# Spare TensorE products in two stretches of a decoder block: an S4D convolution by Fourier products, cross attention, and a gated and expert feed-forward

## The reference

```python
# 1. S4D: a long convolution, by Fourier transforms of length 2048
K = 2 * real(einsum('hn,hnl->hl', Ct, exp(dtA * l)))       # taps, 256 channels x 1024
y = irfft(rfft(x, 2048) * rfft(K, 2048))[:, :1024]
r = x + (y + x * D)
x = layernorm(x + layernorm(r) * ln_w + ln_b)
# 2. cross attention, 16 heads of 16 channels, 77 keys per sequence
x = layernorm(x + softmax(q @ k.T * HD**-0.5) @ v @ Wo.T + bo)
# 3. gated feed-forward (256 -> 1024 -> 256) plus 1024 experts chosen by product keys
mlp = (silu(x @ Wg + bg) * (x @ Wu + bu)) @ Wd + bd
experts = sum over 4 heads and 8 choices of silu(x . down) * softmax(score) * up
x = layernorm(x + mlp + experts)
```

## Time and profile before

| | |
|---|---|
| median of three runs | 738.25 us (733.1 to 738.47) |
| the profiled execution | 737.21 us |
| its span, first to last instruction | 735.4 us |
| TensorE (products) busy | 635.6 us, 86% of the span |
| VectorE busy | 506.9 us, 69% |
| ScalarE busy | 407.0 us, 55% |
| GpSimd busy | 263.6 us, 36% |
| granted TensorE clock, mean | 0.896 of full speed |
| DRAM read and written | 25.47 MB and 13.63 MB |

### The profile page before, as it was taken

One profiled execution on the slowest core, in us unless ns is written; L12 is line 12 of the kernel. 1 busy time (PEld: TensorE's weight loads), 2 busy tenths in 40 slices (PEclk: granted clock), 3 DMA queues, 4 the chain that ended last, 5 costly groups with the idle time before them and its releaser, 6 DMA issues.

```text
span 735.4 us, 8935 instructions
## 1 busy us (share of the span) xinstructions
PE 635.6 (86%) x2724; PEld 425.6 (58%) x2724; DVE 506.9 (69%) x1051; ACT 407.0 (55%) x613; POOL 263.6 (36%) x337
## 2 busy tenths in 40 slices
PE   5698379893849687899999999999999999999996
PEld 2398244581737355554567765567765558654485
DVE  7999937340414578778785787786687877766783
ACT  4852335512113333568875487875487876478660
POOL 0030000075423233554334364334364235445261
PEclk9755579997878755799999999999999999999999
DMA  8909914838990700000000000000000000000000
GB/s 249 353 11 107 112 11 116 159 115 156 118 228 1 285 0 1 0 2 1 0 1 1 0 16 8 7 2 0 1 16 8 8 1 0 8 14 8 0 8 21
DMA packets 31162, 39.67 MB, mean 54 GB/s; under 512 B 3069, under 2 KB 24139, under 8 KB 30091
## 3 DMA queue, kind: packets, MB, share of 16 engines
q1 hardware_dynamic: 26730, 34.91, 22.4%
q10 hardware_dynamic: 4384, 4.20, 1.9%
HBM read 25.47 MB, written 13.63 MB: 53 GB/s over the span
## 4 chain that ended last, share of the span: by engine, by line
PE 61%; DVE 19%; DMA 8%; ACT 5%; issue 4%; SPq 1%; POOL 1%; DVEq 0%; ACTq 0%; POOLq 0%
PE bank L761 19%; PE bank L849 7%; PE bank L854 7%; DMA arena<-scr_x 5%; PE bank L804 3%; PE bank L826 3%; PE bank L783 3%; PE bank L816 3%; PE bank L792 2%; DVE stats L1349 2%; PE bank L648 2%; DVE arena L1440 1%; PE bank L841 1%; PE bank L651 1%; ACT arena L1064 1%
## 5 line engine op out<-in xcount | busy, mean ns | idle before, releaser
L1155 POOL TENSOR_TENSOR arena<-arena 128x1024 f32<-128x1024 f32 x64 | 125.6, 1962 | 157.1 <-ACT arena L1064 156.0
L761 PE MATMUL bank<-arena 128*128 128x512 f32 x384 | 174.5, 596 | 5.9 <-issue 3.6
L761 PEld LDWEIGHTS bank<-arena 128*128 128x128 f32 x384 | 70.0, 190 | 83.6 <-issue 76.6
L1064 ACT ACTIVATE arena<-arena 128x1024 f32<-128x1024 f32 x64 | 73.5, 1149 | 7.5 <-DVE arena L1438 3.2
L1066 ACT ACTIVATE arena<-arena 128x1024 f32<-128x1024 f32 x64 | 73.5, 1149 | 2.1
L1440 DVE SCALAR_TENSOR_TENSOR arena<-arena 128x1024 f32<-128x1024 f32 x48 | 63.8, 1330 | 1.7
L849 PE MATMUL bank<-arena 128*128 128x256 f32 x256 | 58.4, 381 | 2.5 <-DVE tok L1476 1.2
L1330 DVE TENSOR_TENSOR arena<-arena,bank 128x512 f32<-128x512 f32 x36 | 23.1, 684 | 50.4 <-PE bank L651 33.8
L854 PE MATMUL bank<-arena 128*128 128x256 f32 x256 | 57.9, 379 | 0.0
L954 ACT COPY arena<-bank 128x512 f32<-128x512 f32 (+1 forms) x64 | 34.0, 532 | 42.6 <-PE bank L753 30.2
L849 PEld LDWEIGHTS bank<-arena 128*128 128x128 f32 x256 | 47.5, 190 | 10.3 <-issue 3.3
(11 more groups left out here) (182 smaller groups left out, 1221.3 us busy)
## 6 DMA issues: line engine op xcount, KB each, us to landing
scr_x<-arena SPq DMA_DIRECT2D x16, 256.0 KB, 8.0
arena<-scr_x SPq DMA_DIRECT2D x8, 512.0 KB, 21.7
arena<-scr_z SPq DMA_DIRECT2D x32, 128.0 KB, 7.4
scr_z<-arena ACTq DMA_DIRECT2D x14, 256.0 KB, 4.1
tok<-in_x SPq DMA_DIRECT2D x8, 256.0 KB, 5.9
scr_k<-arena SPq DMA_DIRECT2D x4, 512.0 KB, 4.0
arena<-scr_k SPq DMA_DIRECT2D x16, 128.0 KB, 5.7
out<-tok SPq DMA_DIRECT2D x16, 128.0 KB, 1.7
```

Of the source, the lines that this page charges most:

```text
L761: ins = mm(bk[:, :], w[:, k, P * m:P * m + P], src[:, k, :], start=(k == 0), stop=(k == KC - 1))
L1064: fn(ebuf[m % 2], sxb[m % 2], ACT.Prelu, bias=negt[:, n % 2, h:h + 1], alpha=FAR).then_inc(s_ranked, 1)
L1155: tt(sxb[m % 2], sim[:, n % 2, h, 0:XR].unsqueeze(2).broadcast_to((P, XR, NKEYS)), sim[:, n % 2, FH + h, :].unsqueeze(1).broadcast_to((P, ...
```

## The change

Two places get products whose results nobody reads. `keep_busy(bk, count)` issues `count` products of `wq[:, 0, 0:128]` with `wq[:, 1, :]` (128 rows, 128 by 256 columns) into the given PSUM bank.

1. In the second half of the taps' spectra (`hf` is 1) each `k_second` and each `inverse` begins with two of them, ahead of its waits, in bank 4. That makes 18 places with 36 products.
2. `with_busy` puts a step "busy" in front of each `score`, `probs`, `attend`, `turno` and `project` of tiles 0 to 3. That makes 32 steps with three products each, 96 in all. Each takes a unit of the wide ring; it is free again when TensorE itself has finished the step.

```diff
+def with_busy(steps):
+    busy = []
+    for y in steps:
+        if y[0] in ("score", "probs", "attend", "turno", "project") and y[1] < SUPER:
+            busy.append(("busy", len(busy)))
+        busy.append(y)
+    return busy
...
-        PLAN = order(SCHEDULE, "pe")
+        PLAN = with_busy(order(SCHEDULE, "pe"))
...
-                    W_FREE.append((s_wdve, DVE_TURN[key]) if key in DVE_TURN else (s_wact, ACT_TURN[key]))
+                    if part_ == "b":
+                        W_FREE.append((s_wmm, wide_count))
+                    else:
+                        W_FREE.append((s_wdve, DVE_TURN[key]) if key in DVE_TURN else (s_wact, ACT_TURN[key]))
...
             def k_second(hf, k1):
+                if hf:
+                    keep_busy(bank[4], 2)
                 pe.wait_ge(s_kb[hf], 16 * NQ)
...
+            def keep_busy(bk, count):
+                for _ in range(count):
+                    ins = mm(bk[:, 0:2 * P], wq[:, 0, 0:P], wq[:, 1, :], start=True, stop=True, skip_group_check=True)
+                return ins
...
             def inverse(hf, k):
                 m = FREQ * hf + k
+                if hf:
+                    keep_busy(bank[4], 2)
                 pe.wait_ge(s_imat, 16)
...
-            for step in order(SCHEDULE, "pe"):
+            for step in PLAN:
                 kind, n = step[0], step[1]
                 if kind == "conv":
                     conv(n)
+                elif kind == "busy":
+                    keep_busy(w_unit(step + ("b",)), 3).then_inc(s_wmm, 1)
```

More of the change, by code:

```diff
@@ L440, in build @@
         SCHEDULE = plan()
-        PLAN = order(SCHEDULE, "pe")
+        PLAN = with_busy(order(SCHEDULE, "pe"))
         T_AT = {step: u for u, step in enumerate(y for y in PLAN if y[0] in ("turn1", "turn2", "probs", "turno"))}
-        PARTS = {"query": "a", "sim": "a", "expert": "a", "inner": "aA", "spread": "d", "outer": "o", "conv": "a"}
+        PARTS = {"query": "a", "sim": "a", "expert": "a", "inner": "aA", "spread": "d", "outer": "o", "conv": "a", "busy": "b"}
         ACT_TURN = {step + ("a",): u + 1 for u, step in enumerate(
```

## The result

| | before | after |
|---|---|---|
| median of four runs each | 737.32 us | 758.23 us |
| ratio, with its 95% interval | | 1.0295 [1.0252, 1.0338] |
| span of the profiled execution | 735.4 us | 756.2 us |
| TensorE (products) busy | 635.6 us | 674.6 us |
| VectorE, ScalarE, GpSimd busy | 506.9, 407.0, 263.6 us | 507.0, 407.2, 263.9 us |

What follows compares the result with a forecast made beforehand. TensorE was taken to bound the spectra and, with spare products at full clock, attention. The profiled 737.2 us plus 9.7 for the later `conv` and 6.0 for attention gave 752.9, stated as 753.5 us, range 747 to 762.

Steps and rivals of the forecast that it cites:

- The spectra: Second half of the spectra: spare pairs add their time to TensorE, moving its end from 210.25 to 223.5 us.
- The tail: From the last inverse to the first `conv`: shrinks from 10.36 to 6.8 us, so `conv` starts 9.7 us later.
- Attention: Attention of tiles 0 to 3: 77.7 us in all at full clock, 6.0 us longer than now.
- The 32 spare steps: In attention: 32 steps of three spare products cost 41.5 us at full clock.
- The waits: In attention: waits of TensorE that spare products do not cover come on top, 4.7 us.
- its own rule: In attention: a wait longer than the 1.3 us of spare products put ahead of it leaves the excess.
- real work: In attention: the stretch's own products, without spare ones, take 31.5 us at full clock.
- The claim on the clock: In attention: TensorE hardly waits with the spare steps, so its clock is full throughout, 1.00.
- The clock does not hold: In attention: 64-row `score`, narrow `attend` products and transposes let the clock fall; 763 us, chance 0.12.
- Attention comes out even: Attention lasts 70 to 72 us, leaving only the loss in the spectra; 745 to 747 us, chance 0.08.
- The spare products are cheap: In attention: a spare product costs about 0.216 us, so the change pays; 735 us, chance 0.03.
- Its break-even: In attention: below 0.81 us per spare step, 0.27 us a product, the kernel is faster.

Runs made afterwards that it cites:

- 28 and 20: Kernel before plus 28 spare products ahead of the second half's first second stage and 20 ahead of the first `conv`, none elsewhere: 0.9998 [0.9962, 1.0034].
- 33 and 24: Kernel before plus 33 spare products ahead of the second half's first second stage and 24 ahead of the first `conv`, none elsewhere: 0.9973 [0.9948, 0.9997].
- 33 alone: Kernel before plus 33 spare products ahead of the second half's first second stage, none elsewhere: 0.9997 [0.9976, 1.0017].
- 24 alone: Kernel before plus 24 spare products ahead of the first `conv`, none elsewhere: 0.9967 [0.9947, 0.9986].

## Why the prediction was right, point by point

The forecast was 753.5 us, 747 to 762, slower; it was 758.2, inside the range and just above the 749 to 758 that had most of the chance. Against the two profiles, 15.7 us were forecast and 20.8 measured. (752.9 and 1.0 make 753.9 and not 753.5; nothing hangs on it.)

**The spectra, right.** TensorE's end was to move by 13.3 us and moved by 13.6. The pairs until inverse 9 cost 2.0 us instead of 1.7, and the 14 behind them 11.6 as forecast. Runs with one and two products give the same price, 0.43 us each.

**The tail, right in sum, not in its parts.** Forecast 6.8 us, measured 7.17. The last store took 4.0 us until its load could be issued (2.5 forecast, 2.1 and 6.15 were the bounds), and the load 2.6 instead of 3.7. `conv` came 10.5 us later instead of 9.7.

**From `conv` to attention, missed, and the 1.5 us are chance.** The sum had no term for this stretch, and it got 1.5 us shorter: 22.2 instead of 23.7, with a clock of 0.93 in 231 to 253. Not the shorter wait ahead of it did this, since runs with waits of 10.1 to 10.9 us took 22.0 to 22.2 too; the profile of before has the longest such stretch of all. It runs its first 6 us at half clock, and filling the wait ahead brought it to 20.5 to 20.7 us.

**Attention, right in kind, half in size.** 77.7 us were forecast and 83.6 measured, 11.8 longer instead of 6.0. Three terms were too small. The 32 spare steps, each from its start to the start of the next real step without waits, take 45.0 us instead of 41.5: 1.39 to 1.47 us rather than 1.30 beside the score products (1.55 and 1.57 in front of the first two waits), and 2.68 once at half clock. The waits are 5.5 instead of 4.7 (0.79, 1.84, 0.32, 0.62, 0.73, 0.42 and 0.78), near enough, with some luck. The prediction calls 2.28, 2.99 and 4.53 us the longest waits of before and passes over one of 2.45 us, ahead of the second score of tile 2; by its own rule 1.15 us of it should have stayed, and none did. The rest, real work, is 33.1 instead of 31.5. The score of 1.22 us at 308.45, in the short fall of the clock, makes 0.4 of the difference, and 1.0 lies in four pieces with a wait in or behind them (`attend` of tile 2, the two last blocks of transposes, `sim`), where the modelled ends reach further.

**The claim on the clock, right for the wrong reason.** "With the spare steps TensorE hardly waits, so I take full clock throughout" would have given the wrong answer for products over 64 rows. The first half of that sentence holds there too (64.00 of 64.00 us busy), and the clock is at 0.50.

**The signs.** Groups 4.35 us apart, the last inverse at 223.9 us and `conv` 7.2 us behind it came as said. The first expert product came at 336.8 us and not near 332, which is the miss in attention. Half clock in attention was named as a sign of being wrong, and it did show, for some 3 of 83.6 us.

**The rivals.** *The clock does not hold* happened only in the one short fall at 306 us, where a third of the stretch was feared. *Attention comes out even* needs fewer products: with one per step it does. *The spare products are cheap* fell: a pair takes 0.86 us. Its break-even was too generous as well. Without the loss in the spectra it would be 1.11 us of spare time per step (71.7 less 31.5 and 4.7, over 32), but two products, 0.86 us, already cost 0.4%, and one is level: waits and work were taken as fixed there, and with fewer products the waits are longer and the clock is not held.

## What to carry to other kernels

A stretch may be shown as "TensorE at 1.2 GHz" and still be no place for spare products: ask for each wait how long it is, put in no more than fits, and none where products already stand back to back (the second half of the spectra lost 13.6 us of TensorE's time and gained next to no clock, since it was at 1.00 from its third microsecond on). Spread evenly, 96 products in attention cost 11.5 us; 53 of them, placed by the waits, made the kernel 7 us faster than before. Where the fast clock soon meets another engine that is nearly always busy, as VectorE here (21 of 24 us), its worth is the distance to that engine and not half of TensorE's time. And before a difference of 1 or 2 us between two profiles is explained, look at the same stretch in other profiles of the same code: here it alone differed by up to 2 us.

## What was not expected of the hardware

- Products over 64 of 128 rows left TensorE at 1.2 GHz for 68 us without a pause, at a place where the same number over 128 rows left it at 2.4 GHz but for one short fall. In the same run the clock later fell at about 367 us with TensorE busy 4.00 of 4.00 us before and behind.
- After 12 us of spare products at full clock, a pause of 2.1 us and the restart behind it were followed by a fall to 1.2 GHz, for some 3 us. Pauses of 1.84 us (the changed kernel, ahead of the first `probs`) and of 1.68 us (the run that filled the waits to the end, ahead of `conv`) passed without a fall. The length of a pause alone does not decide: one of 2.28 us, ahead of the second score, passed in three runs with a fill (28 and 20, 33 and 24, 33 alone) and neither in the kernel before nor in the run with 24 alone, and in the changed kernel the clock fell behind pauses of 0.32 and 0.62 us among the narrow products of `attend`.
- Stores of planes that land in 2.1 us alone take longer beside the loads of the other planes; the last one took 6.1 us before and 4.0 after, and 7.0 in the run that filled the waits to the end. The tail behind the last product got shorter when the products came more slowly: 10.4, 8.9 and 7.2 to 7.4 us for groups 2.62, 3.49 and 4.35 us apart.
